# FIRE attention with transposes five steps behind scores, and a local transformer stream in a new order with Newton's step on GpSimd

## The chip, the core and the metric

The kernel runs on one core of a Trainium2 chip. The metric is the device time of one execution in microseconds (us), the median of several runs. An execution also taken by the hardware profiler gives the trace from which all rows below come. The engines are TensorE (PE, its weight loads PEld), VectorE (DVE), ScalarE (ACT), GpSimd (POOL) and SyncE (SP, which issues the DMAs). Each runs its own program in order; they meet only at semaphores.

## What is computed

A small network on x of shape 8 x 256 x 128: a mixture of experts, a gated recurrence, the mixture again, a local transformer of six layers, an attention with FIRE position bias, and the same local transformer again. Cut to the two parts that the change touches:

```python
def attn_layer(x, Wqkv, qs, ksc, Wo):            # local transformer, 16 heads of 64
    q, k, v = heads(x @ Wqkv)
    q = rotate(q / max(norm(q), 1e-12) * qs); k = rotate(k / max(norm(k), 1e-12) * ksc)
    # each window of 32 queries looks at its own and the previous 32 keys
    attn = softmax(where(mask, -big, q @ k.T * 8))
    return (attn @ v) @ Wo
def ffn_layer(x, g, bln, W1, b1, W2, b2):
    a, gate = split(layernorm(x) * g + bln) @ W1 + b1
    return a * gelu(gate) @ W2 + b2
for i in range(6):
    x = attn_layer(shift_tokens(x), ...) + x
    x = ffn_layer(shift_tokens(x), ...) + x

att = softmax(q @ k.T * scale + fire_bias)       # FIRE attention, 16 heads of 8, causal
y = (att @ v) @ Wproj + bproj
```

## The kernel before

The program is a row of phases one after the other. `local_transformer_phase` runs twice (about 654 to 2260 us and 2738 to 4340 us of the trace), `fire_attention_phase` once, between them.

**Local stream.** A layer has 32 units: 8 batches times 4 groups of 4 heads. A unit goes through a software pipeline of slots written out by hand: each engine has a function `slot(L, s)`, called for all 6 x 32 slots and a tail, which issues the steps of several units: u0 is the unit of this slot, u1 that of one slot ago, and so on to u5. The order of the calls in `slot` is the order on that engine. `upto(engine, semaphore, unit)` makes the engine wait until that step is done for that unit; `back(u, k)` is the unit k slots earlier. The steps of a unit, in order of need:

- TensorE `project(u,t)` (q and k, t = 0, 1 for halves of the tokens, each three matmuls of 512 columns since a product is split into high and low parts), ScalarE `square_of`, VectorE `lengths` (sum of squares), `cosine` and `sine` (the rotation, read from PSUM), GpSimd `add_turned` (their sum).
- VectorE `floor` (maximum with 1e-24, tile lt_vm), ScalarE `first_guess` (Ln then Exp, tile lt_y), `newton` (one Newton step for the inverse length, tiles lt_ya, lt_yb, lt_rn, 128 x 16 each, on VectorE, lines 1122 to 1128), GpSimd `normalise_qk`.
- TensorE `turn(u,t)` (four transposes into one PSUM bank, TB), ScalarE `take_turned` (copy to lt_qkT), TensorE `values` (v into the same bank as TB), VectorE `take_values`, SP `spread` (store to v_scratch, two loads by windows).
- TensorE `scores` (64 small matmuls), VectorE `mask_scores` and `maxima`, ScalarE `exponentials` (eight, with sums), VectorE `inverse_sums`, GpSimd `normalise_weights`, TensorE `turn_weights`, ScalarE `take_weights`, TensorE `weigh` (64 small matmuls), ScalarE `take_output`, TensorE `merge`, and after four groups VectorE `update_x`.
- GpSimd `next_batch` splits the next batch of x into high and low parts, every fourth slot.

The feed-forward part works on pairs of batches, one in eight slots, by `chunk(L, s, after)`: `mean`, `deviation`, `variance` and the inverse deviation, `normalise`, `high` and `low`, then `gate` (three), gelus, `linear` (three), `product`, `down`, `update`. All its PSUM results but one gate share one bank, F_. ScalarE loads another activation table before and after the gelus. Weights of the next layer are rounded by `high_group` (ScalarE) and their rests taken by `low_group` (GpSimd) in slots 30 to 33.

Scores and outputs share banks 3 and 4, so `scores(u)` waits for `take_output` of the unit three back, and `weigh` for `mask_scores` of a younger unit.

**FIRE stream.** 96 steps, 12 in a batch, each one tile of four heads times 128 keys or two times 256. SIM, PTR, PVS, OTT, OTR and YPR are by how many steps each part lags. Every fourth step TensorE computes four `scores` and VectorE adds their bias (four times), then takes one `maximum` a step; GpSimd subtracts it, ScalarE takes the exponential. TensorE's order in a step is `turn_weights` (PTR behind), scores, `project`, `turn_output`, `turn_heads`, `weigh` (PVS behind). ScalarE's order is the heads' copy, the copy of turned weights of step n - PTR (line 1633), the exponential of step n (line 1639), and the tile's end.

Of the kernel before, what the change touches and what calls it, by code (L numbers as in the profile page):

```python
# [12 lines left out]
P = 128  # L13
# [494 lines left out]
def local_transformer_phase(nc, res, d, X):  # L508
# [8 lines left out]
    with ExitStack() as ctx:  # L517
# [214 lines left out]
        with nc.Block() as block:  # L732
            @block.sync
            def _(sp):
# [11 lines left out]
                def reload(layer, s):  # L746
# [17 lines left out]
                    if later and s == 15:  # L764
                        sp.wait_ge(fhd, layer * (3 * NP))
                        load_columns(sp, fvl, "lt_fv", layer, 3, fvlld)
# [17 lines left out]
            def _(pe):  # L784
# [100 lines left out]
                def variance(c):  # L885
                    upto_pair(pe, fdev, c, 1, 1)
# [18 lines left out]
                def linear(c, k):  # L905
# [5 lines left out]
                    else:  # L911
                        upto_pair(pe, flog, pair(c[0], c[1] + 1), 1, 1)
# [4 lines left out]
                def down(c):  # L917
                    upto_pair(pe, fhd, c, 3, 3)
# [7 lines left out]
                def slot(L, s):  # L926
                    u0, u1, u2, u4, u5 = unit(L, s), unit(L, s - 1), unit(L, s - 2), unit(L, s - 4), unit(L, s - 5)
                    c = chunk(L, s, 17)
                    if c:
                        gate(c, 1)  # L930
# [6 lines left out]
                    c = chunk(L, s, 17)  # L937
                    if c:
                        gate(c, 2)
                    c = chunk(L, s, 23)  # L940
                    if c:
                        down(c)
                    if u2:
                        turn(u2, 0)
                    c = chunk(L, s, 17)
                    if c:
                        linear(c, 0)
                    c = chunk(L, s, 18)
                    if c:
                        linear(c, 1)  # L950
                    if u5:
                        weigh(u5)
                    c = chunk(L, s, 14)
                    if c:
                        variance(c)
                    if u2:
                        turn(u2, 1)
                    if u4:
                        turn_weights(u4)
                    if u5:  # L960
                        merge(u5)
                    if u2:
                        scores(u2)
                    c = chunk(L, s, 16)
                    if c:
                        gate(c, 0)
                    if u1:
                        values(u1)
                    c = chunk(L, s, 22)
                    if c:  # L970
                        linear(c, 2)
# [3 lines left out]
            def _(act):  # L975
# [56 lines left out]
                def gelus(c):  # L1032
                    if c[1] == 0:
                        act.wait_ge(fvgld, c[0] * 16 + 16)
                    for k, (o, n) in enumerate(DB):
                        upto_pair(act, fg, c, (1, 2, 3)[k], 3)
# [814 lines left out]
```

## Time and profile before

| | us |
|---|---|
| median of 3 runs | 4401.52 (4401.02 to 4403.06) |
| the profiled execution | 4395.94 |
| its span, first to last instruction | 4394.2 |

| engine | busy us | share of span |
|---|---|---|
| TensorE | 3849.0 | 88% |
| VectorE | 3408.9 | 78% |
| ScalarE | 3185.7 | 72% |
| GpSimd | 2692.8 | 61% |

TensorE's mean granted clock is 0.936 of full speed. The shares are means over phases with different limits: the page's row of 40 slices shows VectorE at nine tenths or more in the two local streams only. A matmul's end is modelled, and rows of TensorE overlap, so that its lines add to more than its busy time; where its pace matters, the distance from one start to the next tells more. How one reads the rows: the time before the bar is the engine's busy time, the mean of one instruction in ns; behind the bar is what the engine idled before these instructions, and who released it.

### The profile page before, as it was taken

The page shows a single profiled execution, that of the slowest core. Times are in us where ns is not written, and L with a number is a line of the kernel's source. Part 1 is how long each engine was busy: PE and PEld are TensorE (multiplying, and loading weights), DVE is VectorE, ACT ScalarE, POOL GpSimd, SP SyncE. Part 2 cuts the span into 40 slices and gives each one's busy share as a digit, 9 for nine tenths or more (in the row PEclk, how much of TensorE's full clock was granted, in tenths as well). Part 3 has the DMA queues.
Part 4 walks back from the last instruction along what each step waited for, and adds up shares of the span by engine and source line. Part 5 has one row for each costly group of instructions (what it writes and reads, how often), then busy time and mean ns, then how long its engine had stood idle before and what let it go on. Part 6 is the DMA issues. An engine that isn't in the chain of part 4 may idle for free. (4 is left out here: it accounts for less than half of the span.)

```text
span 4394.2 us, 163943 instructions
## 1 busy us (share of the span) xinstructions
PE 3849.0 (88%) x64208; PEld 2781.2 (63%) x64208; DVE 3408.9 (78%) x6643; ACT 3185.7 (72%) x10371; POOL 2692.8 (61%) x2514
## 2 busy tenths in 40 slices
PE   7966968999999999999966665899999999999996
PEld 3423427777777777777745443777777777777773
DVE  1122129999999999999945444999999999999994
ACT  3443437888888888888843433788888888888884
POOL 1110128777777777777723332778777777877772
PEclk8987989999999999999976776999999999999997
DMA  1101113333333333333310000333333333333331
GB/s 58 58 15 44 58 47 103 114 103 117 102 117 104 104 117 105 115 96 109 117 33 7 1 1 33 103 118 103 116 100 117 103 107 114 104 117 96 109 117 39
DMA packets 549312, 377.94 MB, mean 86 GB/s; under 512 B 32576, under 2 KB 533056, under 8 KB 546240
## 3 DMA queue, kind: packets, MB, share of 16 engines
q1 hardware_dynamic: 548560, 367.57, 27.8%
q8 instruction: 514, 8.42, 0.8%
q14 instruction: 238, 1.95, 0.1%
HBM read 265.37 MB, written 102.11 MB: 84 GB/s over the span
## 5 line engine op out<-in xcount | busy, mean ns | idle before, releaser
L1266 POOL TENSOR_TENSOR lt_t<-lt_t 128x512 f32<-128x512 f32 x768 | 973.4, 1289 | 566.9 <-DVE lt_t L1100 566.9
L1002 ACT ACTIVATE lt_pb<-lt_pb,lt_mx 128x64 f32<-128x64 f32 x3072 | 1023.7, 346 | 0.0
L1272 POOL TENSOR_TENSOR lt_t<-lt_t,lt_rn 128x512 f32<-128x512 f32 x768 | 810.9, 1076 | 116.9 <-DVE lt_rn L1128 115.6
L49 PE MATMUL ps<-lt_wh,lt_xh 128*128 128x512 f32 (+1 forms) x1536 | 580.2, 378 | 150.5 <-DVE lt_t L1100 88.7
L1002 ACT ACTIVATION_READ_ACCUMULATOR lt_pb<-lt_pb,lt_mx 128x1 f32 x3072 | 611.5, 199 | 0.0
L984 ACT ACTIVATE lt_qkT<-ps 128x512 f32<-128x512 f32 x768 | 459.0, 598 | 196.5 <-PE ps L804 196.1
L1111 DVE TENSOR_REDUCE lt_ss<-lt_sq 128x8 f32<-128x512 f32 x768 | 518.3, 675 | 14.1 <-ACT lt_sq L979 10.1
L1100 DVE TENSOR_TENSOR lt_t<-ps,lt_tab 128x512 f32<-128x512 f32 x768 | 522.3, 680 | 2.9
L1106 DVE TENSOR_TENSOR lt_t<-ps,lt_tab 128x512 f32<-128x512 f32 x768 | 520.9, 678 | 2.1 <-PE ps L804 0.8
L51 PE MATMUL ps<-lt_wh,lt_xl 128*128 128x512 f32 (+1 forms) x1536 | 522.4, 340 | 0.0
L50 PE MATMUL ps<-lt_wl,lt_xh 128*128 128x512 f32 (+1 forms) x1536 | 521.0, 339 | 0.0
L804 PE MATMUL ps<-ident,lt_t 128*128 128x128 f32 x3072 | 482.1, 280 | 35.1 <-ACT lt_qkT L984 25.4
L979 ACT ACTIVATE lt_sq<-ps 128x512 f32<-128x512 f32 x768 | 452.5, 589 | 69.2 <-PE ps L51 68.6
L49 PEld LDWEIGHTS ps<-lt_wh,lt_xh 128*128 128x128 f32 x1536 | 289.6, 189 | 269.5 <-issue 151.5
L804 PEld LDWEIGHTS ps<-ident,lt_t 128*128 128x128 f32 x3072 | 355.4, 141 | 160.2 <-issue 106.7
L862 PEld LDWEIGHTS ps<-lt_pT,lt_vw 64*64 64x64 f32 x24576 | 398.0, 135 | 88.3 <-issue 88.0
L862 PE MATMUL ps<-lt_pT,lt_vw 64*64 64x32 f32 x24576 | 440.0, 221 | 3.1 <-issue 3.1
L1278 POOL TENSOR_TENSOR lt_pb<-lt_pb,lt_rd 128x512 f32<-128x512 f32 x384 | 400.6, 1043 | 29.9 <-DVE lt_rd L1145 26.9
L876 PE MATMUL ps<-lt_oT,lt_wo 128*128 128x256 f32 x1536 | 405.0, 386 | 1.4 <-ACT lt_oT L1014 1.4
L372 POOL TENSOR_TENSOR M<-M,moe_tmp 128x512 f32<-128x512 f32 x64 | 80.9, 1264 | 511.2 <-DVE moe_tmp L354 511.2
L354 DVE SCALAR_TENSOR_TENSOR moe_tmp<-ps,moe_bb,moe_cbc 128x512 f32<-128x512 f32 x64 | 48.0, 750 | 421.4 <-PE ps L306 421.4
L832 PEld LDWEIGHTS ps<-lt_qkT 64*32 64x32 f32 x24576 | 270.1, 105 | 136.2 <-issue 133.7
(200 smaller groups left out, 7823.6 us busy)
## 6 DMA issues: line engine op xcount, KB each, us to landing
lt_vw<-v_scratch SPq DMA_DIRECT2D x768, 256.0 KB, 3.8
v_scratch<-lt_vv SPq DMA_DIRECT2D x384, 256.0 KB, 2.1
lt_wraw<-in_lt_wqkv SPq DMA_DIRECT2D x56, 384.0 KB, 5.7
moe_cbc<-comb_scratch SPq DMA_DIRECT2D x16, 1024.0 KB, 6.5
moe_w<-in_moe_w SPq DMA_DIRECT2D x32, 256.0 KB, 2.8
lt_wo<-in_lt_wo SPq DMA_DIRECT2D x48, 128.0 KB, 3.7
lt_w<-in_lt_w SPq DMA_DIRECT2D x12, 341.0 KB, 4.5
lt_w<-in_lt_w SPq DMA_DIRECT2D x12, 192.0 KB, 4.1
```

Source lines behind the costliest of these rows:

```text
L49: nc.tensor.matmul(out, lh, rh, start=start, stop=False)
L50: nc.tensor.matmul(out, lh, rl, start=False, stop=False)
L51: return nc.tensor.matmul(out, ll, rh, start=False, stop=stop)
L804: ins = nc.tensor.transpose(TB[:, q * P:(q + 1) * P], t1[:, u[1] % 2, t, q * P:(q + 1) * P], ident[:, :])
L862: ins = nc.tensor.matmul(OR[r][64 * e:64 * e + 64, t * P + w * WIN:t * P + w * WIN + WIN], vw[h, k, 4 * t + w, e * DH:(e + 1) * DH], pT[h, ...
L984: nc.scalar.activation(qkT[:, u[1] % 2, :, WIN + t * P:WIN + (t + 1) * P], TB.rearrange("p (a n) -> p a n", a=4), ACT.Copy).then_inc(tE[t], 1)
L1002: ins = nc.scalar.activation(p, p, ACT.Exp, bias=mx[:, par, c:c + 1], accum_out=sm[:, par, c:c + 1])
L1100: nc.vector.tensor_tensor(o4, a4[:, :, :, ::-1, :], s4, ALU.mult).then_inc(rotd[t], 1)
L1106: nc.vector.tensor_tensor(t1[:, u[1] % 2, t, :].rearrange("p (w h c) -> p w h c", w=2, c=DH), A[t][:, :].rearrange("p (w h c) -> p w h c", ...
L1111: nc.vector.tensor_reduce(ss[:, u[1] % 2, 8 * t:8 * t + 8], sq[:, t, :].rearrange("p (h c) -> p h c", c=DH), AX.X, ALU.add).then_inc(ssd[t ...
L1266: nc.gpsimd.tensor_tensor(o, o, t2[:, t, :], ALU.add).then_inc(padd[t], 1)
L1272: nc.gpsimd.tensor_tensor(o, o, rn[:, u[1] % 2, 8 * t:8 * t + 8].unsqueeze(2).to_broadcast([P, 8, DH]), ALU.mult).then_inc(qkd[t], 1)
```

## The change

In FIRE attention the lags of all parts behind scores grow by three steps (PTR 2 to 5, and so on). In the local stream Newton's step goes from VectorE to GpSimd, as four tensor-tensor operations of 128 x 16 instead of three of which one was fused; a constant tile of 3.0 is added. The orders within the slots of all five engines are written anew, with waits to match: some steps come one slot later or earlier than before. On GpSimd `low_group` runs in slots 31 to 34, one behind its rounding on ScalarE, and on SP `spread` is for u2. Nothing is left out of what is computed.

```diff
 SP
-                    u1 = unit(L, s - 1)
+                    u2 = unit(L, s - 2)
-                    if u1:
-                        spread(u1)
-                stream(sp, slot, 1)
+                    if u2:
+                        spread(u2)
+                stream(sp, slot, 2)
 TensorE: turn, values, slot (order only; c = chunk(L, s, n))
                     if t == 0:
-                        upto(pe, vE, u)
+                        upto(pe, vE, back(u, 1))
...
                 def values(u):
-                    upto(pe, tE[1], back(u, 1))
+                    upto(pe, tE[1], u)
...
-   gate(17,1) mean(13) project(u0,0) project(u0,1) gate(17,2) down(23) turn(u2,0) linear(17,0) linear(18,1)
-   weigh(u5) variance(14) turn(u2,1) turn_weights(u4) merge(u5) scores(u2) gate(16,0) values(u1) linear(22,2)
+   down(23) turn_weights(u5) linear(18,0) mean(13) project(u0,0) project(u0,1) linear(18,1) turn(u2,1) weigh(u5)
+   gate(17,1) gate(17,0) linear(21,2) variance(14) values(u2) scores(u2) merge(u5) gate(17,2) turn(u1,0)
 ScalarE: slot
-   high(16) gelus(17) high_up square_of(u0,0) square_deviation(14) take_turned(u2,0) square_of(u0,1)
-   take_output(u5) take_turned(u2,1) inverse_deviation(14) take_weights(u4) exponentials(u3,0)
-   exponentials(u3,1) first_guess(u0)
+   high_up take_weights(u5) high(16) square_deviation(14) square_of(u0,0) first_guess(u1) take_turned(u2,1)
+   square_of(u0,1) take_output(u5) inverse_deviation(14) exponentials(u3,0) gelus(17) exponentials(u3,1)
+   take_turned(u1,0)
 VectorE: floor, slot
                 def floor(u):
+                    upto(dve, rnd, back(u, 2))
...
-   maxima(u3) newton(u1) product(17,0) normalise(15) lengths(u0,0) cosine(u0,0) lengths(u0,1) sine(u0,1)
-   floor(u0) update_x(u5) sine(u0,0) cosine(u0,1) product(18,1) take_values(u1) product(22,2)
-   mask_scores(u2) deviation(13) inverse_sums(u3) update(23)
+   product(18,0) lengths(u1,0) deviation(13) normalise(15) lengths(u1,1) inverse_sums(u4) floor(u1)
+   product(20,1) maxima(u3) update(23) cosine(u0,0) sine(u0,0) take_values(u2) cosine(u0,1) sine(u0,1)
+   product(21,2) update_x(u5) mask_scores(u2)
 GpSimd: newton, slot
+                def newton(u):
+                    par = u[1] % 2
+                    upto(pool, y0d, u)
+                    nc.gpsimd.tensor_tensor(ya[:, par, :], y0[:, par, :], y0[:, par, :], ALU.mult).then_inc(newt, 1)
+                    upto(pool, newt, u, 1, 3)
+                    nc.gpsimd.tensor_tensor(yb[:, par, :], ya[:, par, :], vm[:, par, :], ALU.mult).then_inc(newt, 1)
+                    upto(pool, newt, u, 2, 3)
+                    nc.gpsimd.tensor_tensor(ya[:, par, :], yb[:, par, :], res["three"][:, :], ALU.subtract).then_inc(newt, 1)
+                    upto(pool, newt, u, 3, 3)
+                    nc.gpsimd.tensor_tensor(rn[:, par, :], ya[:, par, :], y0[:, par, :], ALU.mult).then_inc(rnd, 1)
-   low(16) low_up normalise_qk(u1,0) normalise_qk(u1,1) add_turned(u0,0) add_turned(u0,1)
-   normalise_weights(u3) next_batch(u0) low_group(30 to 33)
+   low_group(31 to 34) low_up normalise_qk(u2,1) next_batch(u0) add_turned(u1,1) normalise_weights(u4)
+   low(16) newton(u1) normalise_qk(u1,0) add_turned(u0,0)
 FIRE attention
-        SIM, PTR, PVS, OTT, OTR, YPR = 0, 2, 3, 4, 5, 6
+        SIM, PTR, PVS, OTT, OTR, YPR = 0, 5, 6, 7, 8, 9
```

Not shown: `next_batch` is called one slot later in its batch (u[1] % GJ == 2), SP reloads the bias of the linears in slot 14 instead of 15, `turn(u,0)` of a layer's first unit also waits for `take_turned` of the unit before, and the waits of `variance`, `linear(2)` and `down` name the step that now stands before them on the bank F_; the gelus wait for the gates in the order 1, 0, 2.

The slots' orders are written here as one line of calls each, feed-forward steps with the slot number that `chunk` gives them, in the order in which the engine issues them.

## Rows read from the trace of the kernel before

**Rows 1.** Windows: us; busy us (x count) of PE, PEld, DVE, ACT, POOL; PEclk; DMA.
```profile
2860.00:4180.00 1320.00, 1251.84 (x25563) 979.08 (x25556) 1279.38 (x2526) 1154.07 (x4061) 1030.75 (x967) 1.00 0.37 109
...
2396.00:2700.00 304.00, 209.92 (x1448) 121.91 (x1448) 128.32 (x238) 121.88 (x240) 97.34 (x96) 0.72 0.00 1
```

**Rows 2.** Lines of DVE, 2860 to 4180 us: busy us, mean ns | idle before.
```profile
L1140 DVE TENSOR_REDUCE lt_mx<-lt_pb 128x8 f32<-128x512 f32 x160 | 108.7, 679 | 0.6
...
L1124 DVE TENSOR_TENSOR lt_yb<-lt_ya,lt_vm 128x16 f32<-128x16 f32 x160 | 102.6, 641 | 5.5
...
L1122 DVE TENSOR_TENSOR lt_ya<-lt_y 128x16 f32<-128x16 f32 x160 | 76.0, 475 | 0.0
...
L1128 DVE SCALAR_TENSOR_TENSOR lt_rn<-lt_yb,lt_y 128x16 f32<-128x16 f32 x160 | 41.0, 256 | 5.5
...
L1117 DVE TENSOR_TENSOR lt_vm<-lt_ss,tiny 128x16 f32<-128x16 f32 x161 | 39.2, 243 | 0.0
```

**Rows 3.** Source L1124, whole run: ns min/median/max, first and last start.
```profile
L1124 DVE TENSOR_TENSOR lt_yb<-lt_ya,lt_vm x384: 174/961/1734, 660.8 to 4306.7; 128x16 f32<-128x16 f32 x192
```

**Rows 4.** Timeline, two engines at one time: start us, us, instruction.
```profile
3285.50 1.04 POOL L1278 TENSOR_TENSOR lt_pb<-lt_pb,lt_rd 128x512 f32<-128x512 f32 x1
...
3285.61 0.96 DVE L1124 TENSOR_TENSOR lt_yb<-lt_ya,lt_vm 128x16 f32<-128x16 f32 x1
```

**Rows 5.** Lines of POOL, 2860 to 4180 us.
```profile
L1266 POOL TENSOR_TENSOR lt_t<-lt_t 128x512 f32<-128x512 f32 x320 | 405.7, 1289 | 234.7 <-DVE lt_t L1100 234.7
...
L1245 POOL TENSOR_TENSOR lt_xl<-lt_xc,lt_xh 128x256 fp32r<-128x256 f32 x40 | 29.2, 730 | 3.2
```

**Rows 6.** Timeline of PE, one plain slot and the down projection before it.
```profile
3307.43 2.81 PE L923 MATMUL ps<-lt_hh,lt_w 128*128 128x512 f32 x6
...
3310.08 0.60 PE L804 MATMUL ps<-ident,lt_t 128*128 128x128 f32 x4
...
3315.19 0.40 PE L49 MATMUL ps<-lt_wh,lt_xh 128*128 128x512 f32 x1
...
3316.58 0.60 PE L804 MATMUL ps<-ident,lt_t 128*128 128x128 f32 x4
```

**Rows 7.** Timeline of PE, scores at the ends of slots, eight slots.
```profile
3273.31 0.86 PE L832 MATMUL ps<-lt_qkT 64*32 64x64 f32 x64
...
3281.15 0.86 PE L832 MATMUL ps<-lt_qkT 64*32 64x64 f32 x64
...
3288.07 0.86 PE L832 MATMUL ps<-lt_qkT 64*32 64x64 f32 x64
...
3303.67 0.86 PE L832 MATMUL ps<-lt_qkT 64*32 64x64 f32 x64
...
3313.59 0.86 PE L832 MATMUL ps<-lt_qkT 64*32 64x64 f32 x64
...
3320.18 0.86 PE L832 MATMUL ps<-lt_qkT 64*32 64x64 f32 x64
...
3338.84 0.86 PE L832 MATMUL ps<-lt_qkT 64*32 64x64 f32 x64
```

**Rows 8.** Lines of ACT, 2860 to 4180 us.
```profile
L984 ACT ACTIVATE lt_qkT<-ps 128x512 f32<-128x512 f32 x320 | 191.3, 598 | 80.1 <-PE ps L804 79.9
...
L990 ACT ACTIVATE lt_y<-lt_vm 128x16 f32<-128x16 f32 x161 | 33.6, 208 | 10.7 <-DVE lt_vm L1117 10.7
```

**Rows 9.** Waits, 2200 to 2760 us: us in total, times, longest.
```profile
DVE fa_nd L1663 <- PE ps L1564: 77.3, 24, 5.1
```

**Rows 10.** Timeline of the FIRE stream, one batch of 12 steps.
```profile
2503.46 1.14 PE L1564 MATMUL ps<-fa_kz,fa_qT 32*128 32x512 f32 x8
...
2509.38 0.58 ACT L1633 ACTIVATE fa_pT<-ps 128x512 f32<-128x512 f32 x1
...
2514.05 1.14 PE L1564 MATMUL ps<-fa_kz,fa_qT 32*128 32x512 f32 x8
...
2541.01 1.14 PE L1564 MATMUL ps<-fa_kz,fa_qT 32*128 32x512 f32 x8
```

More of the change, by code:

```diff
@@ L763, in reload @@
                         load_columns(sp, fvg, "lt_fv", layer, 6, fvgld)
-                    if later and s == 15:
+                    if later and s == 14:
                         sp.wait_ge(fhd, layer * (3 * NP))
@@ L917, in down @@
                 def down(c):
[L918 removed]
+                    upto_pair(pe, flog, pair(c[0], c[1] + 1), 1, 1)
                     if c[1] == 0:
@@ L950, in slot @@
                         linear(c, 1)
+                    if u2:
+                        turn(u2, 1)
                     if u5:
                         weigh(u5)
+                    c = chunk(L, s, 17)
+                    if c:
+                        gate(c, 1)
+                    c = chunk(L, s, 17)
+                    if c:
+                        gate(c, 0)
+                    c = chunk(L, s, 21)
+                    if c:
+                        linear(c, 2)
                     c = chunk(L, s, 14)
@@ L956, in slot @@
                     if u2:
-                        turn(u2, 1)
-                    if u4:
-                        turn_weights(u4)
+                        values(u2)
+                        scores(u2)
                     if u5:
                         merge(u5)
-                    if u2:
-                        scores(u2)
-                    c = chunk(L, s, 16)
+                    c = chunk(L, s, 17)
                     if c:
-                        gate(c, 0)
+                        gate(c, 2)
                     if u1:
[L968 to L971, printed above, removed]
+                        turn(u1, 0)
                 stream(pe, slot, 16)
@@ L1046, in slot @@
                         high(c)
-                    c = chunk(L, s, 17)
-                    if c:
-                        gelus(c)
-                    if s == 15 and running(L):
-                        high_up(act, L)
-                    if u0:
-                        square_of(u0, 0)
                     c = chunk(L, s, 14)
@@ L1232, in slot @@
                         update(c)
+                    if u0:
+                        cosine(u0, 0)
+                        sine(u0, 0)
+                    if u2:
+                        take_values(u2)
+                    if u0:
+                        cosine(u0, 1)
+                        sine(u0, 1)
+                    c = chunk(L, s, 21)
+                    if c:
+                        product(c, 2)
+                    if u5 and u5[1] % GJ == GJ - 1:
+                        update_x(u5)
+                    if u2:
+                        mask_scores(u2)
                 dve.wait_ge(fvlld, 16)
@@ L1286, in slot @@
                 def slot(L, s):
-                    u0, u1, u3 = unit(L, s), unit(L, s - 1), unit(L, s - 3)
+                    u0, u1, u2, u4 = unit(L, s), unit(L, s - 1), unit(L, s - 2), unit(L, s - 4)
+                    if next_layer(L, s, 31, 0) is not None:
+                        low_group(pool, next_layer(L, s, 31, 0), 0)
+                    if next_layer(L, s, 31, 1) is not None:
+                        low_group(pool, next_layer(L, s, 31, 1), 1)
+                    if next_layer(L, s, 31, 2) is not None:
+                        low_group(pool, next_layer(L, s, 31, 2), 2)
+                    if next_layer(L, s, 31, 3) is not None:
+                        low_group(pool, next_layer(L, s, 31, 3), 3)
+                    if s == 15 and running(L):
+                        low_up(pool, L)
+                    if u2:
+                        normalise_qk(u2, 1)
+                    if u0:
+                        next_batch(u0)
+                    if u1:
+                        add_turned(u1, 1)
+                    if u4:
+                        normalise_weights(u4)
                     c = chunk(L, s, 16)
@@ L1717, in program @@
         tiny = sb("tiny", [P, 16])
+        three = sb("three", [P, 16])
         rank = sb("rank", [P, TILES, EXPERTS])
```

135 lines of the change are left out of this document (50 added, 85 removed).

## The prediction, made before the changed kernel ran

> **What bounds the kernel now.** I read the busy time by stage first, then the groups of instructions by line in a stretch of full work, then the order of time slot by slot. Two stages are touched by the change: the two streams of the local transformer (384 slots in all, some 3,200 us) and the FIRE attention stream (96 steps, some 300 us). In 1320 us of the second local stream VectorE is busy for 1279.4 us (97%), TensorE for 1251.8, ScalarE for 1154.1, GpSimd for 1030.8 [rows 1]. The groups of that stretch count 160 units [rows 2], so a slot takes 1320 / 160 = 8.25 us, with 8.00 us of VectorE, 7.82 of TensorE, 7.21 of ScalarE and 6.44 of GpSimd in it. VectorE sets the pace, but TensorE is only 0.43 us a slot behind the end. In time order that 0.43 isn't spread evenly: a plain slot is dense on TensorE (transposes at 3310.08 and again at 3316.58, 6.50 us) [rows 6], and the loss lies in slots that carry feed-forward work. Eight slots, the work of one pair of batches, took 3338.84 - 3273.31 = 65.5 us from scores to scores [rows 7]; the two with gates and linears took 18.66 of them (from 3320.18), the one with the down projection 9.92 (3303.67 to 3313.59), a plain one 6.6.
>
> A sixth of VectorE's time goes into Newton's step: three operations on 16 columns. Their rows add 102.6 + 76.0 + 41.0 = 219.6 us, with 11 us of gaps 230.6, or 1.44 us a slot [rows 2]. That is not their work: the second one takes 174 ns at its shortest and 961 ns at its median [rows 3]. Two lines of time show why [rows 4]: it begins at 3285.61, GpSimd has been on its weights' normalisation since 3285.50, and they end at 3286.57 and 3286.54. A VectorE operation with two SBUF inputs stands still here until GpSimd's running one has ended.
>
> **Newton's step leaves VectorE.** VectorE's busy time falls by 219.6 / 160 = 1.37 us a slot to 6.63. What that can give is what TensorE has idle, 384 x 0.43 = 165 us: the cap of this part.
>
> **Newton's step on GpSimd.** Four operations of 128x16 instead of three (the fused one is split; the 3.0 comes from a new tile). The trace shows no such small tensor-tensor operation on GpSimd. 128x512 takes 1289 ns and 128x256 takes 730 [rows 5], so a column costs 2.18 ns and the fixed part is 0.17 us: 16 columns make 0.21 us, and I add 0.07 for the semaphore between dependent ones. Ends: 4 x 0.17 = 0.7 us, and 4 x 0.73 = 2.9 us if each costs like 256 columns. I take 4 x 0.28 = 1.1 us, by the fit. GpSimd goes from 6.44 to 7.55 us a slot, just under TensorE. Its order becomes normalise_qk(u2,1), add_turned(u1,1), normalise_weights(u4), newton(u1), normalise_qk(u1,0), add_turned(u0,0). Behind newton's new wait for the first guess is queued what turn(u1,0), at the end of TensorE's slot, needs. From a plain slot's start on TensorE: project(u0,0) ends at 1.2, its square at 1.8, the guess at 2.4, newton at 3.5, normalise at 4.6; the transpose is due at 6.05. So the wait has 1.4 us of cover; without it each microsecond is one on TensorE.
> The Trainium skill (GPSIMD Engine Reference, section 4.1, Engine selection) speaks against this edit: elementwise work belongs on VectorE, GpSimd being about 2 times slower with two inputs. No row shows it for 16 columns; an estimate by that page, twice the 174 ns, is 0.35 us each, 1.4 us in all, and GpSimd would stand at 7.84 us, level with TensorE. The same page (section 1, Specifications) says that the SBUF interfaces are shared when VectorE has two SBUF inputs; by that rule, the trace agrees (0.96 us instead of 0.17).
>
> **The new order.** Transposes of q and k are split (t=0 at the end of a slot, t=1 in the next), lengths, floor and guess go one slot later, the first linear to slot 18, the third to 21, product 1 to 20, weights' transposes to u5, mask and values come into one slot. ScalarE, TensorE and SP get no work added. SP's store of v and its two loads go one slot later, as their source does and as weights' transposes do: same cover, cost nothing. Low parts of the weights (4 operations a layer on GpSimd) go one slot behind the roundings: nothing, or 2 us a layer if GpSimd is full. One wait gets tight: scores(u2) needs take_output(u5), which needs weigh(u5) of the same slot, and only values (0.7 us, half of the two projects from 3315.19 to 3316.58 [rows 6]) lies between; ScalarE's copy of 0.6 [rows 8] just fits if ScalarE is free. Queued behind are merge and the next transpose.
> I laid the eight slots on these terms. By slot modulo 8, now and then: 0: 6.6 to 7.3 (GpSimd has low and the next batch near); 1 and 2: 18.7 to 17.6 (TensorE needs 2 x 6.50 + 5 products of 0.70 = 16.5; two table loads and three gelus on ScalarE hold the rest); 3: 7.8 to 6.9; 4: 6.9 to 7.2; 5 and 6: 15.6 to 15.9 (the third linear is in 5 now); 7: 9.9 to 9.3 (TensorE 6.50 + 2.65 for down [rows 6]). Sum 64.2, against 65.5 in this stretch and 66.0 (8 x 8.25) in the mean. Times 48 groups: 62 to 86 us; I take 75.
>
> **FIRE attention.** VectorE waits 77.3 us there for scores [rows 9], which are queued behind transposes that wait for fresh exponentials. With five steps between they don't. But on ScalarE the copy of transposed weights goes ahead of the exp in each step, so the copy of n-4 stands behind exp(n). In time: scores at 2503.46, the first copy behind the new exp at 2509.38, 5.92 later, the next scores at 2514.05 [rows 10]. TensorE now stops at the transpose of n, about 6 us after scores, and has T W T W T (T transposes, W weigh) to do before the next; afterwards it stops at weigh(n-4), 6.6 after scores, with W T W T to do. One T saved (0.6), 0.5 later: nothing. And the tile ends move: the turned heads now wait behind two exps, and VectorE's update for ysb ahead of the second maximum. By hand at full clock a batch of 12 steps comes to 33.5 us before and 33.9 after; measured it is 2541.01 - 2503.46 = 37.55, at a granted clock of 0.72 in the stage [rows 1], and I see no reason for another share of slow clock. 8 x 0.4 = 3 us, and 1 for three more steps of drain: +4 us, at most +30 with the clock lower.
>
> **Sum.** Profiled execution 4395.9 us (span 4394.2, 1.7 around it) - 75 + 4 = 4325. The median of the runs, 4401.5, lies 5.6 above it: 4330 us.
>
> **Rivals.** (1) TensorE at its cap and FIRE freed. For: if FIRE closed up to TensorE's work (210 of 304 us busy [rows 1]) it would give up to 94 us. With local -165 and FIRE -40: 4191, or 4196 for the median. Against: ScalarE's order above, and heavy slots that are of different engines.
> (2) Slower, by a loop through the shared port. Floor is still a two-input operation on VectorE and lies in a loop now: floor, guess, copy of turned(u2,1), values, take_values, cosine, sine, mask, two lengths, floor. Six VectorE passes at 0.6 to 0.68 [rows 2], floor 0.1, guess 0.5, copy 0.6, values 0.7, handovers 0.7: 6.3 us plus floor's wait for GpSimd. Floor takes 243 ns on average now [rows 2], but GpSimd will be busy for over 90% of a slot. With 0.4 of wait the loop is 6.7, near TensorE's 6.5; with a whole add_turned (1.29 [rows 5]) 7.6 in plain slots. It decides from about 0.9 us of mean wait. Five of eight slots 0.8 longer than laid out are 64.2 + 4 = 68.2, 48 x 2.2 = 106 us above now: 4507. For it: the guess already waits for floor, 10.7 us in 160 slots [rows 8].
> (3) GpSimd takes VectorE's place: newton at 0.48 us an operation makes it 6.44 + 1.9 = 8.35 us a slot, and nothing is won: 4400 to 4440.
>
> **Chances and range.** Forecast (some 25 to 130 us won) 0.55; (1), more than 130, 0.12; (2) 0.17; (3) 0.16, half of it still a small gain. That gives faster by over 0.2% (9 us, about what a measurement here can tell from no change) 0.75, within 0.08, slower 0.17. The range reaches into (1) and over (3): 4220 to 4440.
>
> **What would show it.** Right: VectorE below 85% busy in the local streams and TensorE near 97%; the four newton operations on GpSimd at 0.2 to 0.3 us each, GpSimd near 92%; gates' slots at 17.6; FIRE's batch near 37 us, its wait for scores smaller and ScalarE's for the subtraction as large. Wrong: FIRE's batch at 30 us or less; newton's operations near 0.5 us; floor at 0.7 us with ScalarE's guess waiting for it in every slot; plain slots above 7.3 us.

## The result and the profile after

The changed kernel takes 4560.3 us (median of 4 runs, 4559.4 to 4568.3) beside 4401.3 for the kernel before: a ratio of 1.037, 95% interval 1.036 to 1.038. It is 159 us slower where 71 us faster was forecast. One of the four runs of one experiment below (merge ahead of scores and no low parts) took 8296.9 us and is left out of its median. The profiled execution has a span of 4566.5 us. Its engines, from the page:

```profile
PE 3921.2 (86%) x64208; PEld 2886.5 (63%) x64208; DVE 3036.6 (66%) x5491; ACT 3199.8 (70%) x10371; POOL 2992.2 (66%) x4049
```

VectorE lost 372 us of busy time and GpSimd gained 299, as intended. The window of full work that answers to [rows 1] (busy us of each engine, granted clock, DMA):

```profile
2860.00:4180.00 1320.00, 1221.59 (x24528) 979.54 (x24527) 1074.43 (x1953) 1105.21 (x3883) 1105.19 (x1545) 0.97 0.39 104
```

155 units pass here instead of 160. No engine is above 93%, while VectorE stood at 97% before. So nothing is full, and the time must lie in waits and in what follows from them. The groups by line that answer to [rows 2, 5, 8] (busy us and mean ns of one; behind the bar idle time before them):

```profile
L1120 DVE TENSOR_TENSOR lt_vm<-lt_ss,tiny 128x16 f32<-128x16 f32 x155 | 64.5, 416 | 0.3 <-issue 0.3
L1265 POOL TENSOR_TENSOR lt_yb<-lt_ya,lt_vm 128x16 f32<-128x16 f32 x155 | 34.6, 223 | 12.1
L1263 POOL TENSOR_TENSOR lt_ya<-lt_y 128x16 f32<-128x16 f32 x155 | 33.8, 218 | 15.7 <-ACT lt_y L994 15.7
L991 ACT ACTIVATE lt_y<-lt_vm 128x16 f32<-128x16 f32 x155 | 33.1, 214 | 42.7 <-DVE lt_vm L1120 42.1
```

Newton's operations are 0.22 us on GpSimd. The waits of the same window: total us, times and longest. In the trace of before, the second and third don't occur in this window, and the fourth is 0.8 us:

```profile
DVE lt_vv L1142 <- PE ps L51: 156.1, 131, 5.9
POOL lt_wl L602 <- ACT lt_wh L596: 53.5, 16, 8.6
PE ps L806 <- POOL lt_t L1275: 48.5, 31, 3.8
PE ps L834 <- issue: 24.8, 28, 1.8
```

GpSimd waits in `low_group` (L602) for ScalarE's rounding; TensorE waits in `turn` (L806) for GpSimd's normalise_qk; and TensorE stands in `scores` (L834) for nothing that the profile names ("issue"). VectorE's wait for v (L1142, 14.9 us before) is idle time of an engine that is now busy for 81% of the window.

**Where in a layer it went.** The distance from the first scores of a stream to its last, summed over both streams, was 3121.1 us and is 3277.0: 156 us. (Another 14 us passed between the streams, where FIRE lies, and 3 behind the last scores; this profiled execution took 8 us more than the median run.) By groups of eight slots, mean of layers 2 to 5 of both streams:

| group of a layer | 1 | 2 | 3 | 4 | layer |
|---|---|---|---|---|---|
| before, us | 65.4 | 66.0 | 64.1 | 68.0 | 263.6 |
| after, us | 66.0 | 67.8 | 65.1 | 80.2 | 279.0 |

The third group is the least disturbed. Its slots, at the median, take 64.4 us before (6.8, 6.8, 7.9, 7.7, 9.9, 6.6, 11.5, 7.2) and 64.3 after (6.5, 6.6, 8.5, 7.6, 9.1, 6.9, 8.5, 10.6); I call that a quiet group. So at its best the new order is level with the old one. Over both streams the first three groups lost 41 us, and the fourth, in which the next layer's weights are rounded, 118: 11.8 at each of ten ends (a stream of six layers has five).

The layer's end in order of time, GpSimd, ScalarE, then TensorE, of the changed kernel:

```profile
3082.16 1.29 POOL L1258 TENSOR_TENSOR lt_t<-lt_t 128x512 f32<-128x512 f32 x1
3084.36 1.82 POOL L602 TENSOR_TENSOR lt_wl<-lt_wraw,lt_wh 128x768 fp32r<-128x768 f32 x1 [0.91 <-ACT lt_wh L596]
3086.13 1.05 POOL L1275 TENSOR_TENSOR lt_t<-lt_t,lt_rn 128x512 f32<-128x512 f32 x1
```

```profile
3082.95 0.60 ACT L985 ACTIVATE lt_qkT<-ps 128x512 f32<-128x512 f32 x1
3083.44 0.84 ACT L596 ACTIVATE lt_wh<-lt_wraw 128x768 fp32r<-128x768 f32 x1
```

```profile
3084.36 0.39 PE L51 MATMUL ps<-lt_wh,lt_xl 128*128 128x512 f32 x1
3087.23 0.66 PE L806 MATMUL ps<-ident,lt_t 128*128 128x128 f32 x4 [2.49 <-POOL lt_t L1275]
```

ScalarE's high_group (L596) begins at 3083.44, because it is behind take_turned(u1,0) (L985), which needs the last step of TensorE's slot. GpSimd comes to low_group before it is done, waits 0.91 us, computes 1.82, and only then does normalise_qk(u2,1), which TensorE's turn(u2,1) of the next slot needs. TensorE stands 2.49 us. Such a chain TensorE, ScalarE, GpSimd, TensorE can close in each of the four slots of a layer's end. In the whole run GpSimd waits for a rounding 44 times, 144.3 us; in the kernel before it was 2 times, 6.6 us. The last of the four waits of an end is the longest, 5.9 to 8.6 us in this stream, because there ScalarE's rounding also stands behind the gelus and their two table loads of 1.28 us:

```profile
3112.08 1.81 POOL L602 TENSOR_TENSOR lt_wl<-lt_wraw,lt_wh 128x768 fp32r<-128x768 f32 x1 [8.60 <-ACT lt_wh L596]
```

**What a wait costs besides its length.** The next 5 us behind those 2.49, and the first stream from its first scores to its last, first before, then after:

```profile
3087.00:3092.00 5.00, 4.77 (x139) 4.22 (x139) 1.07 (x3) 3.62 (x16) 4.69 (x9) 0.66 0.04 8
```

```profile
670.94:2231.08 1560.14, 1476.69 (x30277) 1156.95 (x30277) 1507.45 (x2978) 1361.90 (x4794) 1214.69 (x1139) 1.00 0.37 109
```

```profile
670.35:2312.40 1642.05, 1508.31 (x30263) 1207.46 (x30262) 1323.34 (x2408) 1366.36 (x4796) 1363.48 (x1900) 0.97 0.39 103
```

The granted clock is 0.66 there, and weigh's 64 matmuls at 3087.82 take 1.60 us; elsewhere in this trace 1.14 is usual. Over the stream the clock is 0.97 instead of 1.00, and practically the same matmuls keep TensorE busy for 32 us more; in both streams together 65 of the 156 us are of this kind. A matmul's end is modelled, so the split is rough, but a wait of TensorE at a layer's end costs more than its own length.

### The profile page after: what moved, and what is told of

Its sections match the earlier page's. It is cut to its first block and busy times, and to the rows that moved or that the text cites. A ratio compares the mean times of both kernels' runs of the same rounds, so it can differ in the third digit from the quotient of the medians.

```text
span 4566.5 us, 163940 instructions
## 1 busy us (share of the span) xinstructions
PE 3921.2 (86%) x64208; PEld 2886.5 (63%) x64208; DVE 3036.6 (66%) x5491; ACT 3199.8 (70%) x10371; POOL 2992.2 (66%) x4049
## 5 line engine op out<-in xcount | busy, mean ns | idle before, releaser
L1258 POOL TENSOR_TENSOR lt_t<-lt_t 128x512 f32<-128x512 f32 x768 | 993.4, 1294 | 19.2 <-DVE lt_t L1102 19.2
L49 PE MATMUL ps<-lt_wh,lt_xh 128*128 128x512 f32 (+1 forms) x1536 | 606.2, 395 | 77.8 <-POOL lt_xl L1237 57.4
L985 ACT ACTIVATE lt_qkT<-ps 128x512 f32<-128x512 f32 x768 | 452.2, 589 | 256.1 <-PE ps L806 247.7
L806 PE MATMUL ps<-ident,lt_t 128*128 128x128 f32 x3072 | 479.0, 279 | 144.4 <-POOL lt_t L1275 133.1
L1003 ACT ACTIVATION_READ_ACCUMULATOR lt_pb<-lt_pb,lt_mx 128x1 f32 x3072 | 591.7, 193 | 0.0
L806 PEld LDWEIGHTS ps<-ident,lt_t 128*128 128x128 f32 x3072 | 377.4, 143 | 283.8 <-POOL lt_t L1275 186.8
L1142 DVE COPY lt_vv<-ps 128x512 f32<-128x512 f32 x384 | 265.1, 690 | 406.0 <-PE ps L51 405.0
L1113 DVE TENSOR_REDUCE lt_ss<-lt_sq 128x8 f32<-128x512 f32 x768 | 494.9, 676 | 0.0
L878 PE MATMUL ps<-lt_oT,lt_wo 128*128 128x256 f32 x1536 | 453.2, 419 | 8.0 <-ACT lt_oT L1015 4.2
L864 PE MATMUL ps<-lt_pT,lt_vw 64*64 64x32 f32 x24576 | 452.8, 224 | 5.7 <-issue 5.7
L864 PEld LDWEIGHTS ps<-lt_pT,lt_vw 64*64 64x64 f32 x24576 | 409.9, 139 | 72.7 <-issue 72.5
L834 PE MATMUL ps<-lt_qkT 64*32 64x64 f32 x24576 | 355.6, 230 | 76.0 <-issue 65.6
```

Source lines behind the costliest of these rows:

```text
L49: nc.tensor.matmul(out, lh, rh, start=start, stop=False)
L806: ins = nc.tensor.transpose(TB[:, q * P:(q + 1) * P], t1[:, u[1] % 2, t, q * P:(q + 1) * P], ident[:, :])
L864: ins = nc.tensor.matmul(OR[r][64 * e:64 * e + 64, t * P + w * WIN:t * P + w * WIN + WIN], vw[h, k, 4 * t + w, e * DH:(e + 1) * DH], pT[h, ...
L1003: ins = nc.scalar.activation(p, p, ACT.Exp, bias=mx[:, par, c:c + 1], accum_out=sm[:, par, c:c + 1])
L1113: nc.vector.tensor_reduce(ss[:, u[1] % 2, 8 * t:8 * t + 8], sq[:, t, :].rearrange("p (h c) -> p h c", c=DH), AX.X, ALU.add).then_inc(ssd[t ...
L1258: nc.gpsimd.tensor_tensor(o, o, t2[:, t, :], ALU.add).then_inc(padd[t], 1)
```

## The experiments

Theory: the time is lost at the layer's end, by low_group standing ahead of normalise_qk(u2,1) on GpSimd. Rivals: Newton's step is dearer on GpSimd than on VectorE (its wait, or the loop through floor); FIRE's new lags; the new order as such. Times are medians; the ratio is to the kernel before.

**Low parts moved back, by the text.** The changed kernel with low_group as the last call of slots 30 to 33, as before.

```diff
-                    if next_layer(L, s, 31, 0) is not None: ...      # head of GpSimd's slot
                     if u0:
                         add_turned(u0, 0)
+                    if next_layer(L, s, 30, 0) is not None: ...      # its end
```

> The changed kernel with one thing undone: GpSimd's low_group is again the last call of slots 30 to 33 instead of the first call of slots 31 to 34. Theory A (the low parts stand at the head of GpSimd's slot and wait there for ScalarE's rounding, which is the last call of ScalarE's slot before; all of GpSimd's work for the transposes queues behind): the slots at the layers' ends shrink, a layer goes from about 278 to about 263 us, the wait of lt_wl for lt_wh (144 us) falls under 30 us, and the time comes to 4400 to 4440 us. Theory B (GpSimd is simply too full with Newton's step when the low parts come on top): little changes, 4520 to 4560 us.

4564.4 us, 1.038 (1.036 to 1.040): no difference from the changed kernel, and neither of the two theories was tested. The last call of slot 30 and the first call of slot 31 are neighbours in GpSimd's program; the change's "one slot later" moved nothing. What is new is only what stands before and behind it. The same edit the other way round, on the kernel before (low_group at the head of slots 31 to 34):

> The kernel before with only this part of the change: low_group as the first call of slots 31 to 34 of GpSimd. Theory A: the same wait appears and the layers' ends grow here too, by some 5 to 15 us each for 12 ends, 4460 to 4560 us. Theory B: GpSimd has room here, so within 10 us of the kernel before, 4401 us.

4402.4 us, 1.001 (1.000 to 1.002): nothing, for the same reason.

**Low parts truly a slot later.** The changed kernel with low_group as the last call of slots 31 to 34, behind newton, normalise_qk(u1,0) and add_turned.

> The changed kernel with low_group still one slot behind its rounding (slots 31 to 34), but as the last call of GpSimd's slot instead of the first. Theory A says the place in the order costs, not the lag: 4400 to 4440 us, as with both undone. If the lag itself costs (the next layer's projections wait for the low part of their group, that is due at slot 32 to 35), the time stays above 4500 us.

4482.7 us, 1.020 (1.018 to 1.022): 78 us of the 159 are gone, with not one operation less, though the forecast 4400 to 4440 was missed. TensorE's wait in turn for normalise_qk falls from 133.1 us in the whole run to 39.1. A third place, right behind normalise_qk(u2,1):

> The changed kernel with low_group of slots 31 to 34 directly behind normalise_qk(u2,1) on GpSimd instead of at the head. Now in the issue order it can't hold back the transposes of t=1 of that slot, and the rounding it waits for has had 1 us more. Theory A (what costs is that normalise_qk(u2,1) stands behind the wait): at or below the 4483 us of low_group at the slot's end, 4440 to 4485 us. If GpSimd's load at the layers' ends costs (B), 4480 to 4520 us.

4487.2 us, 1.020 (1.019 to 1.022). So it is what low_group stands ahead of that costs, which is what the theory said; but it explains half.

**No low parts.** The changed kernel with the low parts of the weights of layers 2 to 6 not computed (the projections there use old low parts).

> The changed kernel without low_group after the first layer: the low parts of the projection weights are not computed for layers 2 to 6 (those of layer 1 are used), so 20 operations of 1.82 us a phase and their waits on GpSimd are left out. It is the bound of what low_group costs in any place. Theory A: near the best place, 4430 to 4470 us. Theory B: clearly below it, 4400 to 4430 us. What stays above 4401 us is not low_group's.

4422.5 us, 1.005 (1.003 to 1.007). Even without the work the new order is not faster than the old one. This kernel's TensorE shows the next loss:

```profile
2965.18 1.14 PE L865 MATMUL ps<-lt_pT,lt_vw 64*64 64x32 f32 x64
...
2966.94 0.28 PE L51 MATMUL ps<-lt_wh,lt_xl 128*128 128x256 f32 x1
2967.15 0.57 PE L835 MATMUL ps<-lt_qkT 64*32 64x64 f32 x35
2968.99 0.45 PE L835 MATMUL ps<-lt_qkT 64*32 64x64 f32 x29 [1.27 <-issue]
```

After 35 of its 64 small matmuls the scores stop for 1.27 us, and the trace names no semaphore that holds them. In the new order the first of scores' 64 follows 2 us behind the first of weigh's 64, with six matmuls of values between; before, transposes and merge lay between weigh and scores.

**Merge between.** The kernel of "truly a slot later" with TensorE's merge(u5) ahead of scores(u2).

```diff
                         values(u2)
-                        scores(u2)
                     if u5:
                         merge(u5)
+                    if u2:
+                        scores(u2)
```

> The changed kernel with low_group last in slots 31 to 34 (4483 us) and, on TensorE, merge(u5) ahead of scores(u2), both of which wait for the same take_output(u5). Theory C: in the new order 128 matmuls and loads of weigh and 128 of scores come within 3 us, TensorE's instructions run out in the middle of scores (26 us of idle named issue at L834 in 1320 us, 0.8 us before the change), and every fourth slot VectorE's update_x holds mask_scores until merge is through. With merge between, the issue idle at scores falls under 10 us per 1320 and the time by 30 to 70 us, to 4410 to 4455 us. If neither matters: 4475 to 4490 us.

4420.7 us, 1.005 (1.003 to 1.006): 62 us. The stalls in scores of the whole run, before this edit and with it:

```profile
PE ps L834 <- issue: 74.2, 79, 2.1
```

```profile
PE ps L834 <- issue: 14.9, 22, 1.8
```

59 us of stall went and 62 us of time. All that lies between the two runs of small matmuls now, and didn't before, is merge's four matmuls of 256 columns; the work is the same. A rival for the same stall was that scores were late because VectorE's mask of the unit before stands behind update_x; so mask_scores ahead of update_x, in the kernel with merge behind scores:

> The changed kernel with low_group last in slots 31 to 34 (4483 us) and, on VectorE, mask_scores(u2) ahead of update_x(u5). It takes only the second half of theory C: update_x's wait for merge no longer holds mask_scores, lengths, floor and inverse_sums of the next slot. If that wait (17 us of 1320, and GpSimd's wait for lt_rd behind it) costs, 10 to 40 us less: 4440 to 4470 us. If only the instructions' issue costs, 4475 to 4490 us.

4492.3 us, 1.021 (1.019 to 1.023): no gain. VectorE's wait in update_x for merge fell from 59.8 us in the whole run to 26.8, and the stalls in scores stayed at 74.9. That rival falls. Why TensorE stops there the trace doesn't show; it shows that the place in the order decides. Stops of this kind aren't new, either. The kernel before has next to none in scores (2.0 us in the whole run), but 15 in turn_weights, which there come soon behind weigh, up to 2.8 us long:

```profile
PE ps L844 <- issue: 14.3, 15, 2.8
```

**Newton's step alone, in both orders.** First the kernel before with nothing changed but Newton's step, four operations on GpSimd ahead of normalise_qk(u1,0):

> The kernel before with Newton's step alone moved to GpSimd, ahead of normalise_qk(u1,0), no other order touched. VectorE is 97% busy there; if it sets the pace as I read it, 1.4 us of 8.25 leave it and the slot falls towards TensorE's 7.8: 4300 to 4370 us. If the slots are in truth held by TensorE and ScalarE one by one, 4385 to 4415 us. If GpSimd's chain gets late for the transposes, above 4420 us.

4326.3 us, 0.986 (0.979 to 0.993): 75 us faster by the medians, 62 by the ratio, whose interval is 33 to 92, since its four runs spread from 4313.6 to 4374.2. A tighter measure comes below: with FIRE's copies led, the same step takes 4281.0 to 4201.9, 79 us. Its window of full work:

```profile
2860.00:4180.00 1320.00, 1268.75 (x26170) 1003.69 (x26169) 1141.99 (x2097) 1179.94 (x4149) 1192.84 (x1646) 1.00 0.41 111
```

TensorE is at 96%, GpSimd at 90. A quiet group takes 63.2 us, 1.2 less than before, a layer 257.7 (263.6 before), and the two streams from scores to scores 3050.0, 71 less. Then the new order with Newton's step back on VectorE (and low_group truly a slot later, so the comparison is with 4482.7):

> The changed kernel with low_group at the end of slots 31 to 34 (4483 us) and Newton's step back on VectorE, as three operations behind the cosine and sine of t=0. If Newton's step on GpSimd is a gain that the new order hides, this is slower, 4500 to 4560 us; if GpSimd's load of 83% is what costs in the new order (theory B), faster, 4430 to 4470 us.

4530.7 us, 1.029 (1.027 to 1.031): 48 us slower than with it on GpSimd. There the operation behind [rows 3] is not held up:

```profile
L1126 DVE TENSOR_TENSOR lt_yb<-lt_ya,lt_vm 128x16 f32<-128x16 f32 x154 | 31.6, 205 | 5.3
L1119 DVE TENSOR_TENSOR lt_vm<-lt_ss,tiny 128x16 f32<-128x16 f32 x155 | 81.0, 523 | 0.0
```

205 ns instead of 641: from its new place it seldom meets a running operation of GpSimd (175 ns at the median). The move is worth its 48 us all the same. Whether through the work that VectorE is spared or the place of the step in the chain from floor to normalise_qk wasn't tried; GpSimd's normalise_qk waits 622.0 us in the whole run for VectorE's result there (115.6 in the kernel before), so the place is a rival that stands.

**What the order itself costs.** With merge ahead of scores, the new order is still about 90 us above the old one with Newton's step on GpSimd and FIRE's lags. The same omission of low parts was made in both.

> The changed kernel with low_group as the last call of slots 31 to 34 and merge ahead of scores on TensorE (4420.7 us), and low_group left out after the first layer of each phase: the low parts of the later layers' projection weights are not computed. Theory A (the new order's layer end is long because GpSimd makes the low parts there, once TensorE's instructions no longer run out): it measures 4360 to 4375, since without merge's move the same omission was worth 60 us (4482.7 to 4422.5). Theory B (the two costs overlap: both were one wait seen twice): it measures 4405 to 4420. Then the remaining distance of about 90 us to the old order with Newton's step on GpSimd is in the order of the gated layers' and quiet slots themselves: a quiet group of eight slots 64.2 to 65.3 us against 63.2.

4356.9 us, 0.990 (0.988 to 0.992): 64 us less than with them, where it was 60 without merge's move. The two costs are apart.

> The kernel before with Newton's step on GpSimd (4326.3 us) and low_group left out after the first layer of each phase: the low parts of the later layers' projection weights are not computed. In the new order that omission was worth 60 and 62 us. Theory A (the cost of the low parts at the layer's end is made by the new order, which uses both GpSimd and the projection weights closer to each other): here it is worth 0 to 20 us, 4306 to 4330. Theory B (the low parts cost both orders the same, 12 boundaries by some 5 us): it measures 4260 to 4275, and the 90 us between the orders are the new order's own slots.

4295.5 us, 0.978 (0.976 to 0.980): 31 us less than with them, between the two theories: the low parts cost the old order half of what they cost the new one. What is left between the two, without low parts, is 61.4 us. Most of it is in the slots: the first scores of the window and those 128 slots later, first of the new order, then of the old:

```profile
2857.43 0.86 PE L835 MATMUL ps<-lt_qkT 64*32 64x64 f32 x64
3895.94 1.01 PE L835 MATMUL ps<-lt_qkT 64*32 64x64 f32 x64
```

```profile
2855.27 0.86 PE L833 MATMUL ps<-lt_qkT 64*32 64x64 f32 x64
3874.50 0.74 PE L833 MATMUL ps<-lt_qkT 64*32 64x64 f32 x51
```

1038.5 / 4 = 259.6 us a layer against 1019.2 / 4 = 254.8. The four groups of a layer take 64.4, 65.3, 64.6 and 65.0 against 63.3, 63.6, 63.3 and 64.6. From first to last scores the two streams take 3070.7 us against 3022.5, which is 48 of the 61; the rest passes between and behind the streams.

**FIRE.** The kernel before with lags 5 to 9 alone:

> The kernel before with only the FIRE part of the change (lags 5 to 9). My account (the copy of the turned weights stands behind the new exponential on ScalarE, and the tiles' ends wait there too) says 37.5 us a batch becomes 37.5 to 39.5: 4400 to 4420 us. The rival (the bubble at the scores closes) says 4310 to 4360 us.

4403.5 us, 1.001 (1.000 to 1.002): +4 us at the most likely, and no more than 8. The waits in FIRE with the new lags, of this run (window 2396 to 2700, nearly the whole stage):

```profile
ACT fa_nd L1639 <- POOL fa_nd L1544: 145.9, 41, 10.4
DVE fa_nd L1663 <- PE ps L1564: 90.3, 22, 5.9
PE ps L1580 <- ACT fa_oh L1627: 74.2, 16, 6.1
```

In the same window of before they were 127.7, 74.0 and 3.8 us.

ScalarE stands before the exponential (L1639) for GpSimd's subtraction; its copies of what TensorE has finished stand behind it; TensorE waits for such a copy (L1580), and VectorE for the scores behind that. So I led ScalarE's copies: the kernel before with lags 5 to 9, and on ScalarE

```diff
-        SIM, PTR, PVS, OTT, OTR, YPR = 0, 2, 3, 4, 5, 6
+        SIM, PTR, PVS, OTT, OTR, YPR = 0, 5, 6, 7, 8, 9
+        COPY, HEADS_COPY, OUT_COPY, Y_COPY = 3, 5, 7, 8
 # ScalarE's slot
-                    qe = at(n, OTT)
+                    qe = at(n, HEADS_COPY)
-                    q = at(n, PTR)
+                    q = at(n, COPY)
-                    tl = tile_end(at(n, OTR))
+                    tl = tile_end(at(n, OUT_COPY))
-                    tl = tile_end(at(n, YPR))
+                    tl = tile_end(at(n, Y_COPY))
```

> The kernel before with the FIRE lags 5 to 9 (4403 us by itself) and ScalarE's copies called earlier in its order: the turned weights 3 steps behind instead of 5, the heads' copy 5, the output's 7, ysb 8. By my account the copy of step n-4 behind exp(n) is what keeps the batch at 37 us; ahead of it TensorE has work during the whole chain and a batch falls to 24 to 30 us: 8 x 8 to 13 us, 4300 to 4340 us. If something else holds it: 4390 to 4410 us.

4281.0 us, 0.973 (0.972 to 0.975): 118 us from a stage of 300. From first to last scores it takes 163.1 us instead of 285.8, a batch 21.4 instead of 37.6. Its window and waits:

```profile
2396.00:2600.00 204.00, 165.14 (x1472) 94.69 (x1472) 142.85 (x260) 126.81 (x252) 98.58 (x97) 0.94 0.01 1
```

```profile
POOL fa_nd L1545 <- DVE fa_mx L1671: 73.7, 31, 5.6
DVE fa_nd L1664 <- PE ps L1565: 35.9, 23, 3.3
ACT fa_nd L1640 <- POOL fa_nd L1545: 31.4, 33, 12.0
PE ps L1581 <- ACT fa_oh L1628: 12.4, 16, 1.0
```

ScalarE's wait fell from 145.9 to 31.4, VectorE's from 90.3 to 35.9 and TensorE's for the copy from 74.2 to 12.4. TensorE's granted clock is 0.94 where [rows 1] has 0.72: it is at 2.4 GHz, the higher of its two levels, most of the time, and the engine is busy for 165 of 204 us, where it was busy for 210 of 304. Do the copies need the long lags? Lags 2 to 6 with copies 1, 2, 4 and 5 steps behind:

> The kernel before with FIRE's lags as they were (2, 3, 4, 5, 6) and only ScalarE's copies called earlier within that order (the copy of the turned weights one call behind the scores, of the heads' output two, of the turned output four, of the projection five). In the kernel with lags 5 to 9 and the copies led, 118 us went. Theory A (the gain is the copies no longer standing behind TensorE's same-step work on ScalarE, whatever the lags): it measures 4280 to 4310. Theory B (the long lags are needed: with the transposes two steps behind the scores the exponentials and sums of a batch are not done when TensorE comes to its transposes, and the copies then wait as before): it measures 4380 to 4405, and so the change's lags were a precondition of a gain that its unmoved copies kept from it.

4427.9 us, 1.006 (1.004 to 1.007): slower than before, above both theories. TensorE now waits for fresh exponentials in its transposes (window 2396 to 2720; before 31.1 us):

```profile
PE ps L1556 <- ACT fa_nd L1640: 103.6, 55, 4.9
```

So neither half works alone: +4 us for the lags, +25 for the copies, -118 for both.

**The parts together.** Both mends of the local stream and the led copies in the changed kernel:

> The changed kernel with the two mends of its local stream (low_group last in slots 31 to 34, merge ahead of scores; 4420.7 us) and ScalarE's copies in FIRE led by two, two, one and one steps. FIRE and the local stream run in different phases. Theory A (the parts add): 4420.7 minus the 121 us that the led copies took from the kernel before with the same lags (4403.5 to 4281.0) is 4300, range 4290 to 4312. Theory B (the gain in FIRE is partly a gain of clock that the denser stream before it takes back): 4320 to 4360.

4291.5 us, 0.975 (0.973 to 0.976). The parts add (4300 by the sum). And the best of both, the old order with Newton's step on GpSimd, lags 5 to 9 and led copies:

> The kernel before with Newton's step on GpSimd (4326 us alone) and the FIRE stream of the run above. The two are in different phases, so the gains add: 4326 less 60 to 100 us, 4225 to 4265 us.

4201.9 us, 0.955 (0.954 to 0.957): 196 us faster than the kernel before by the ratio, 358 faster than the changed one by the medians, and a little beyond the forecast.

**The account of the change**, from medians. The parts are taken one after the other along one row of kernels, so they add up by construction; in another order a part could have another size.

| part | us | from |
|---|---|---|
| Newton's step on GpSimd, old order | -75 | 4401.3, 4326.3 |
| FIRE's lags | +4 | ratio 1.0009 |
| new order: its slots, and what lies between the streams | +57 | 4295.5, 4356.9, less FIRE's 4 |
| new order: low parts dearer | +33 | 63.8 less 30.8 |
| scores ahead of merge (small matmuls bunched) | +62 | 4482.7, 4420.7 |
| low parts ahead of normalise_qk(u2,1) | +78 | 4560.3, 4482.7 |
| sum | +159 | 4560.3, 4401.3 |

## Why the prediction was wrong

**Newton's step: right.** The forecast was 0.28 us for each operation; the trace has 0.22, begun 0.30 apart, 1.2 us in all against 1.1. VectorE is at 81% (forecast under 85). With that part alone the time fell by 75 us, inside the cap of 165 and near the forecast's whole gain of 75, and rival 3, newton at 0.48 us an operation, fell. That the two numbers agree is chance: the forecast's 75 were meant for this step and the new order together. The Trainium skill (GPSIMD Engine Reference, section 4.1, Engine selection), by which elementwise work goes to VectorE, pointed the wrong way here: an operation is little slower on GpSimd (223 ns, not the 0.35 us estimated by that page, against 174 to 205 unhindered on VectorE), and on VectorE it stood behind GpSimd's running operation at 961 ns median [rows 3]. What the same page says of the shared interfaces (section 1, Specifications) fits those 961 ns, but it isn't the whole gain: in the new order the step met hardly any such wait on VectorE (205 ns), and moving it was still worth 48 us.

**The new order: the step that failed.** The term "48 groups: 62 to 86 us; I take 75" is what failed, and it had two errors. First, the eight slots laid by hand came to 64.2 us, and a quiet group measures 64.3; but this was subtracted from 65.5 and from 66.0, the mean over whole layers. A quiet group of before is 64.4. The stretch of [rows 7], 65.5, is the first group of a layer, with 7.8 where others have 6.8. Like with like, the layout gave 0.2 us a group, 10 us in all. The 75 us were the difference between a layout without a layer's end and a mean with one. And the layout is reached in the quietest group only: in the mean the first three groups became longer, 41 us over both streams.

Second, the layer's end was priced with one sentence, "nothing, or 2 us a layer". Its last eight slots went from 68.0 to 79.8 us, 118 us over ten ends, and 78 of the 159 us go when low_group is called behind normalise_qk. The sentence read the edit by slot numbers; on GpSimd end of slot 30 and head of 31 are the same place. The question was what had come to stand behind low_group (normalise_qk(u2,1), with TensorE due for it at once) and ahead of high_group on ScalarE (take_turned(u1,0), with TensorE's last step ahead of it). Both can be read from the orders of the change; high_group is the last call of ScalarE's slot in both kernels. That waits would also lower TensorE's clock in the local streams, from 1.00 to 0.97, was no term of the sum.

**Why the order gains nothing even in quiet slots.** With Newton's step gone from VectorE, the old order runs a quiet group in 63.2 us by itself, TensorE at 96%. The prediction counted Newton's relief and the new order's layout in one number and never asked what the old order alone would make of the relief. The signs named in advance say the same: TensorE was expected near 97% and is at 92.5% (96% in the old order with Newton's step moved), GpSimd near 92% and is at 84.

**The tight wait that was named, and the one that wasn't.** Scores(u2) behind take_output(u5) was named as tight. What held scores were stops inside its own row of matmuls, 62 us. The trace of before has next to none of them in scores (0.8 us in the window of [rows 1]), but it has them in turn_weights, up to 2.8 us long, and no bound was set for placing 128 small matmuls close together.

**The rivals.** Rival 2 had the sign and, at 4507, lay within 53 us of the result, but by another mechanism. Of its loop, floor did get longer, 416 ns mean from 243, with 177 at the median and 1189 at most:

```profile
L1120 DVE TENSOR_TENSOR lt_vm<-lt_ss,tiny x155: 174/177/1189, 2860.4 to 4177.7; 128x16 f32<-128x16 f32 x155
```

That is 0.24 us of mean wait, and the guess waits 0.27 us a slot for it; the rival was to decide from 0.9. What of the 57 us in the order's slots is due to it wasn't tried. In rival 1 the freed FIRE was bounded at 94 us, against which stood ScalarE's order; that order was the whole obstacle. It was seen and not followed to its end: move the copies, and 118 us are there, more than the bound, which held TensorE's busy time for fixed; it fell by 45 us at the higher clock.

**FIRE: right in the number, in part by luck.** +4 forecast, +4 measured alone (interval 0 to +8). A batch was forecast to get 0.4 us longer and is 37.7 to 40.1, 1.1 longer in the mean; a first batch 7 us shorter pays for it, so that from first to last scores it is 284.9 us against 285.8 (285.0 in the changed kernel). That the step saved on TensorE is lost again on ScalarE was the right reading: TensorE's wait for exponentials in the transposes went from 31.1 us to 0.3, and that for the copied heads came from 3.8 to 74.2. One sign named in advance failed: VectorE's wait for scores was to get smaller and grew from 74.0 to 90.3.

## What to carry to other kernels

When an order written by hand is laid out anew, compare like with like: the new layout of a period against the measured time of the same period, never against a mean that also holds ends of layers. Then lay out the rare slots too; here the eight of 32 that hold a layer's end lost 118 of 156 us. "One slot later" means something only where the call changes its neighbours on its engine: read what is queued behind it and who is waiting for that. And try the parts one by one before the bundle: one part of this change was worth -75 us, and a second became worth -118 when another engine's order followed it.

## What the runs showed of the hardware

Three matters were not expected. TensorE can stand up to 2.7 us in a run of small matmuls while the trace names no semaphore for it: 73 such stalls in scores, 65.6 us in the changed kernel, where another run of 64 small matmuls begins 2 us earlier. In the kernel with low_group moved it was 79 stalls and 74.2 us, and four 256-column matmuls put between the two runs left 22 and 14.9 us.

At the layers' ends TensorE's waits are followed by a lower clock: 0.66 in the 5 us behind a wait of 2.49 us, and 1.60 us for 64 small matmuls that otherwise take 1.14.

And in FIRE the granted clock rose from 0.72 to 0.94 when the waits between TensorE's steps shrank, and the stage's scores took 123 us less from first to last. Of these, 45 us are TensorE's busy time for nearly the same matmuls (209.9 to 165.1 us); how far the clock and the shorter waits brought about each other wasn't separated.
